# Kept orders stored in four parts, record fills and weights spread over six slots, the root's row first

## The reference

```
coeff = complex(x[...,0], x[...,1]) * sqrt_eig                  # 64 x 256 x 257
h = irfft(einsum('nlm,mlk->nkm', coeff, pct), n=512)            # 64 blocks of 256 x 512
a = layernorm(h)
key = a @ K;  logits = tanh(key @ a.T + bias) - 10000*(1-band)  # band: 12 wide
h = h + softmax(logits*temperature) @ a
f = layernorm(h)
h = h + ffn(f)      # ffn: adds one-hot results of a 7-layer net, only at rows where f[0] and f[1] are >= 0.5
```

## Time and profile before

| | us |
|---|---|
| median of three executions | 1478.48 |
| the profiled execution, its time | 1485.5 |
| its span, first to last instruction | 1483.7 |
| TensorE busy | 1341.8 (90%) |
| VectorE busy | 930.9 (63%) |
| ScalarE busy | 900.5 (61%) |
| GpSimd busy | 558.1 (38%) |
| mean granted TensorE clock | 0.962 |

### The profile page before, as it was taken

How to read it: one execution, slowest core, us unless ns; L and a number is a source line. 1 busy time by engine, 2 the same in 40 slices (tenths; PEclk the granted TensorE clock), 3 DMA queues, 4 the chain that set the end, 5 groups by cost and what they waited for, 6 DMA issues and landing times. The chain is left out here.

```text
span 1483.7 us, 30658 instructions
## 1 busy us (share of the span) xinstructions
PE 1341.8 (90%) x8813; PEld 1165.0 (79%) x8813; DVE 930.9 (63%) x2025; ACT 900.5 (61%) x1956; POOL 558.1 (38%) x1394
## 2 busy tenths in 40 slices
PE   4998877884599999999999999999999999799893
PEld 3776666674599999999999999999999988455451
DVE  1222222222488878878887887887888777566661
ACT  1222222221477777777777777777777767567661
POOL 0000000000055555555555555555555556522222
PEclk9999999997799999999999999999999999899996
DMA  9999999969423433333433333333333222100000
GB/s 353 425 422 426 424 426 425 425 266 236 92 80 98 84 82 94 94 81 84 97 82 79 96 82 81 95 86 82 89 96 79 81 55 56 35 8 8 8 3 4
DMA packets 87269, 219.64 MB, mean 148 GB/s; under 512 B 20598, under 2 KB 33538, under 8 KB 75330
## 3 DMA queue, kind: packets, MB, share of 16 engines
q1 hardware_dynamic: 77690, 190.33, 40.5%
q10 hardware_dynamic: 4160, 27.27, 4.4%
q0 software_dynamic: 5376, 1.52, 0.6%
HBM read 147.77 MB, written 72.68 MB: 149 GB/s over the span
## 5 line engine op out<-in xcount | busy, mean ns | idle before, releaser
L589 PE MATMUL ps_k<-sphi,Glo 128*128 128x256 f32 x1024 | 292.2, 285 | 0.0
L588 PE MATMUL ps_k<-splo,Ghi 128*128 128x256 f32 x1024 | 291.0, 284 | 0.0
L587 PE MATMUL ps_k<-sphi,Ghi 128*128 128x256 f32 x1024 | 288.6, 282 | 0.0
L218 PE MATMUL s1b<-pg,cg 128*128 128x256 f32 x1024 | 241.3, 395 | 47.2 <-DVE cg L190 46.1
L218 PEld LDWEIGHTS s1b<-pg,cg 128*128 128x128 f32 x1024 | 199.4, 197 | 91.6 <-issue 29.6
L190 DVE TENSOR_TENSOR cg<-xg,se 128x1024 f32<-128x1024 f32 x64 | 78.4, 1225 | 228.6 <-DMA pg<-in_pct_dram 216.5
L1196 POOL TENSOR_SCALAR ve<-var 128x2 f32<-128x2 f32 x64 | 13.9, 217 | 523.6 <-ACT squares L911 523.5
L587 PEld LDWEIGHTS ps_k<-sphi,Ghi 128*128 128x128 f32 x1024 | 194.7, 190 | 2.4
L588 PEld LDWEIGHTS ps_k<-splo,Ghi 128*128 128x128 f32 x1024 | 193.0, 189 | 2.7
L589 PEld LDWEIGHTS ps_k<-sphi,Glo 128*128 128x128 f32 x1024 | 193.8, 189 | 0.0
L273 ACT COPY stage<-s1b 128x512 f32<-128x512 f32 x104 | 60.8, 585 | 169.9 <-PE s1b L218 167.3
(11 more groups left out here) (171 smaller groups left out, 3162.1 us busy)
## 6 DMA issues: line engine op xcount, KB each, us to landing
pg<-in_pct_dram SPq DMA_DIRECT2D x64, 1024.0 KB, 26.0
xg<-in_xs_dram SPq DMA_DIRECT2D x64, 512.0 KB, 23.7
out_dram<-o SPq DMA_DIRECT2D x64, 512.0 KB
xt<-spec SPq DMA_DIRECT2D x60, 512.0 KB
spec<-stage ACTq DMA_DIRECT2D x52, 512.0 KB, 8.1
rrow<-rs SPq DMA_DIRECT2D x64, 128.0 KB
spec<-hold SPq DMA_DIRECT2D x2, 2880.0 KB, 24.9
recs<-rec SPq DMA_DIRECT2D x16, 160.0 KB, 11.6
```

Source lines behind the costliest of these rows:

```text
L218: last = nc.tensor.matmul(bank[at * PARTS + part][:, m % 2, :], cg[:, b % SETS, m * 2 + h, :], pg[:, b, m * 2 + h, :], start=(h == 0), sto ...
L587: nc.tensor.matmul(out_ap, whi, mhi, start=(j == 0), stop=False)
L588: nc.tensor.matmul(out_ap, whi, mlo, start=False, stop=False)
L589: last = nc.tensor.matmul(out_ap, wlo, mhi, start=False, stop=(j == n - 1))
```

## The change

The first load phase handles three blocks instead of four, and block 3's direct load goes behind the first `rrow` in slot 0. Blocks 4 to 7 are loaded in the direct way too (`load_direct`), in slots 0 to 3. The stores of the kept rows cover blocks 8 to 63, in four parts of 14 blocks with two DMAs each, one part in each of slots 0 to 3. The 16 fills go to slots 0, 1 and 2 (six, six, four), the seven weight loads to slots 4 and 5. The counts that are waited for on `x_loaded` and `hold_stored` follow.

```diff
+DIRECT = 8
+        def loads(n, k):
+            if isinstance(n, int) and n < DIRECT:
+                return 48 * (n // 4 + 1)
+            return n * 4 + (80 - 4 * k)
...
-            for n in range(4):
-                sp.dma_start(xt[0:FROM, n]..., spec[n]...[0:FROM]).then_inc(x_loaded[n], 16)
+            def load_direct(n, k):
+                sp.dma_start(xt[0:FROM, k]..., spec[n]...[0:FROM]).then_inc(x_loaded[k], 16)
                 for c in range(2):
-                    sp.dma_start(xt[FROM:P, n, ...], const.hold[c * NB + n:...]).then_inc(x_loaded[n], 16)
-            for c in range(2):
-                sp.dma_start(spec[4:NB, (c + 1) * NLAT - HELD * GM:(c + 1) * NLAT, :],
-                             const.hold[c * NB + 4:c * NB + NB]).then_inc(hold_stored, 16)
+                    sp.dma_start(xt[FROM:P, k, ...], const.hold[c * NB + n:...]).then_inc(x_loaded[k], 16)
+            def store_held(part):
+                each = (NB - DIRECT) // 4
+                n0 = DIRECT + part * each
+                for c in range(2):
+                    sp.dma_start(spec[n0:n0 + each, (c + 1) * NLAT - HELD * GM:(c + 1) * NLAT, :],
+                                 const.hold[c * NB + n0:c * NB + n0 + each]).then_inc(hold_stored, 16)
+            def empty_records(q0, q1):
+                empty = recs.rearrange("(p q r) w -> p q r w", p=P, r=8)
+                for q in range(q0, q1):
+                    sp.dma_start(empty[:, q], const.rec0[:, :, :]).then_inc(rec_emptied, 16)
+            for n in range(3):
+                load_direct(n, n)
             sp.wait_ge(const.rec_filled, 2)
-            empty = recs.rearrange("(p q r) w -> p q r w", p=P, r=8)
-            for q in range(NB * NLAT // (P * 8)):
-                sp.dma_start(empty[:, q], const.rec0[:, :, :]).then_inc(rec_emptied, 16)
-            for dst, src in ffn_consts:
-                sp.dma_start(dst, src).then_inc(ffn_loaded, 16)
...
                     sp.dma_start(rrow[:, k % 2], rs[i]...).then_inc(rrow_loaded[k % 2], 16)
+                if isinstance(i, int) and i == 0:
+                    load_direct(3, 3)
                 if has(i) and has(i + 4):
                     sp.wait_ge(pe_dft, i * 2 + 2)
                     sp.wait_ge(act_sphi, i + 1)
                     sp.wait_ge(dve_splo, i + 1)
-                    if isinstance(i, int) and i == 0:
-                        sp.wait_ge(hold_stored, 32)
-                    load(i + 4, k)
+                    if isinstance(i, int) and i + 4 < DIRECT:
+                        load_direct(i + 4, k)
+                    else:
+                        if isinstance(i, int) and i + 4 == DIRECT:
+                            sp.wait_ge(hold_stored, 128)
+                        load(i + 4, k)
+                if isinstance(i, int) and 0 <= i < 4:
+                    store_held(i)
+                if isinstance(i, int) and 0 <= i < 3:
+                    empty_records((0, 6, 12)[i], (6, 12, 16)[i])
+                if isinstance(i, int) and 4 <= i < 6:
+                    for dst, src in ffn_consts[(0, 4)[i - 4]:(4, 7)[i - 4]]:
+                        sp.dma_start(dst, src).then_inc(ffn_loaded, 16)
```

More of the change, by code:

```diff
@@ L519, in load @@
                              spec[n].rearrange("(h p q) w -> p h (q w)", h=2, q=2)).then_inc(x_loaded[k], 16)
-            for n in range(4):
-                sp.dma_start(xt[0:FROM, n].rearrange("p (h q) w -> p h (q w)", h=2),
-                             spec[n].rearrange("(h p q) w -> p h (q w)", h=2, q=2)[0:FROM]).then_inc(x_loaded[n], 16)
+            def load_direct(n, k):
+                sp.dma_start(xt[0:FROM, k].rearrange("p (h q) w -> p h (q w)", h=2),
+                             spec[n].rearrange("(h p q) w -> p h (q w)", h=2, q=2)[0:FROM]).then_inc(x_loaded[k], 16)
                 for c in range(2):
-                    sp.dma_start(xt[FROM:P, n, 2 * c:2 * c + 2, :].rearrange("p q w -> p (q w)"),
+                    sp.dma_start(xt[FROM:P, k, 2 * c:2 * c + 2, :].rearrange("p q w -> p (q w)"),
                                  const.hold[c * NB + n:c * NB + n + 1, :, :].rearrange("o (p q) w -> o p (q w)", q=2)
-                                 ).then_inc(x_loaded[n], 16)
-            for c in range(2):
-                sp.dma_start(spec[4:NB, (c + 1) * NLAT - HELD * GM:(c + 1) * NLAT, :],
-                             const.hold[c * NB + 4:c * NB + NB]).then_inc(hold_stored, 16)
-            sp.wait_ge(const.rec_filled, 2)
-            empty = recs.rearrange("(p q r) w -> p q r w", p=P, r=8)
-            for q in range(NB * NLAT // (P * 8)):
-                sp.dma_start(empty[:, q], const.rec0[:, :, :]).then_inc(rec_emptied, 16)
-            for dst, src in ffn_consts:
-                sp.dma_start(dst, src).then_inc(ffn_loaded, 16)
+                                 ).then_inc(x_loaded[k], 16)
+            def store_held(part):
[10 more added lines that the diff above has]
+                load_direct(n, n)
+            sp.wait_ge(const.rec_filled, 2)
             def load_records(s, u):
@@ L615, in inverse_dft @@
             def inverse_dft(n, k):
-                pe.wait_ge(x_loaded[k], n * 4 + (48 - 4 * k))
+                pe.wait_ge(x_loaded[k], loads(n, k))
                 for t in range(TILES):
@@ L823, in slot @@
                     act.wait_ge(ffn_loaded, 16 * len(ffn_consts))
-                    act.wait_ge(hold_stored, 32)
+                    act.wait_ge(hold_stored, 128)
                     nc.scalar.copy(W1h[:, :, :], const.W1f[:, :, :]).then_inc(weight_hi, 1)
@@ L852, in slot @@
                     n, k1 = i + 1, (k + 1) % 4
-                    act.wait_ge(x_loaded[k1], n * 4 + (48 - 4 * k1))
+                    act.wait_ge(x_loaded[k1], loads(n, k1))
                     wait(act, pe_logit, n - 1)
@@ L1013, in slot @@
                 if isinstance(i, int) and i == AHEAD:
-                    dve.wait_ge(hold_stored, 32)
+                    dve.wait_ge(hold_stored, 128)
                     split_weights()
```

## The result

Six executions of each: median 1486.34 us (1484.29 to 1489.4) after, 1479.76 (1477.11 to 1483.5) before, ratio 1.0044, 95% interval 1.0024 to 1.0064. The change costs 6.6 us: small, clear of noise, and just within the 0.5% that I called no change. Forecast: 1481.5, range 1455 to 1494, no change the likeliest.

A forecast was written before the change was run, and what follows sets the result against it. TensorE and VectorE wait for block 0's rrow, issued late behind stores and fills on SyncE. The 36.5 us gained at L0 are given back in slots 0 to 3, plus a 1.0 us cold slot: +3, 1481.5 us, range 1455 to 1494.

The forecast's parts named there:

- The first row: Block 0's rs and rrow go out right after its root, rs at 338.9, making its lsc 36.5 us earlier.
- L0: Start of VectorE's lsc of block 0: 383.58 before, forecast 347.1.
- The price of a part: Slots 0 to 3: two stores of 14 adjacent partitions, 7.3 us each, 14.5 us a part.
- Rival B: A part costs its bytes, 7.4 us; fills' issue sets slots 0 and 1; steps 20.3, 17.7, 13.8; 1462; chance 0.20.
- The fills: Slots 0 to 2, six, six and four: 0.53 us each moved, 2.5 us each to issue while store packets run.
- Rival D: SyncE's issue of fills, 3.1 us each, makes rs late in slots 0 and 1: +13 us, 1491.5; chance 0.13.
- The edits at nothing: Reading blocks 4 to 7 from hold, hold_stored at 128, POOL's wait for fills, waits at slot 60: no cost.
- The steps: Times between lsc of successive blocks: L1 at 372.2, then 22.9, 23.3 and 21.2 us to L4 at 439.6.
- The cold slot: One slot at the end with TensorE cold after idling: 1.0 us, 8.2 against 7.1.
- The total: The whole change: +3 us on the median, 1481.5 us.
- L1 to L4: Starts of lsc of blocks 1 to 4, where 14.8, 7.6, 9.7 and 7.4 us are given back.
- the free case: Nothing else late after the first row: L1 at 357.4, whole gain 37.5 us.

The follow-up runs named there:

- f1: Kernel before with the big stores, all 16 fills and all weights moved behind the first rs and rrow, nothing split: 1476.51 us, ratio 0.9984.
- s1: Changed kernel with each store part taking every fourth block instead of 14 adjacent ones: 1460.29 us, ratio to before 0.9875.
- p0: Kernel before with nine extra stores out of hold, from different sets of partitions, each waited for before the next: 1542.7 us in one execution.
- g1: Changed kernel with fills at three a slot over slots 0 to 5 instead of six, six, four; stores unchanged: 1488.88 us, ratio 1.0057.
- b4: Changed kernel with seven strided parts, the first and block 3's load before rs, 13 fills in the loop, weights in slot 59: 1449.26 us, ratio 0.980.
- q1: Changed kernel with the same store parts and fills issued on GpSimd's queue instead of SyncE's: 1485.56 us, ratio 1.0048.
- b2: Changed kernel with seven parts of every seventh block, one in each of slots 0 to 6, fills three a slot: 1461.93 us, ratio 0.9879.

## Why the prediction was right

- *The first row.* L0 = 347.1 forecast, 347.07 measured; rs at 338.3, 0.6 us before its forecast, and rrow at 341.8. f1 shows that by itself the first row gives little.
- *The price of a part*, 14.5 us instead of the 7.4 of its bytes. This decided, and s1 and p0 show it apart from everything else. It rested on two packets of 1.81 us among those of 3.7. The parts took 15.1 to 15.5 us; in the first the packets of the first store were over after 8.0 us. Rival B's time, 1462, is near the 1460.3 of s1, where a part takes nearly as long as B gave it (7.7 to 8.2 us against 7.4), but its path was another one: it had lsc of block 1 at 369.5 by dearer fills, and s1 had it at 364.3.
- *The fills*, 0.53 us each beside the stores. g1 took half of them out of slots 0 and 1 and was 0.8 us ahead at block 1 (1.1 at block 0) and gained nothing at block 4, less than the 2 us that I expected: it issues three in slot 3, where the changed kernel has none. In the first two slots rrow followed the last store packet by 3.6 and 3.2 us, against 4.7 and 5.2 with six fills: 0.5 us for each fill less.
- *Rival D* was closer than its chance says. It was to decide from 2.3 us a fill, and the fills took 2.7; its sign, rs issued later than the last store packet lands, is there in slot 0 (rs at 364.99, the last packet done at 364.0) and by 0.3 us in slot 1. Only g1 shows that the two bounds lie side by side, and that rs issued earlier brings rrow no earlier.
- *The edits at nothing* held. GpSimd waited once, 9.2 us, for the fills (to 414.2), and the root that it made next, by 418.8, was still ready before SyncE came to its rs at 421.8.
- *The steps.* 25.8, 24.2, 24.1 and 22.0 us measured, 25.1, 22.9, 23.3 and 21.2 forecast: each 0.7 to 1.3 short, 3.4 in sum. From rrow's issue to the first store packet I gave 2.2 + 1 + 0.4 = 3.6 us, and it was 3.6, 3.7 and 3.5 in slots 1 to 3; in slot 0, with two loads, it was 7.1 against 5.9. From the last store packet to rrow's issue it was 4.7, 5.2, 5.2 and 2.8 against 4.7, 4.7, 5.1 and 3.0. The term that was too small is the part itself, by 0.6, 0.9, 1.0 and 0.6 us. In slot 1 its first packet starts at 372.3, most others of the first store at 373.3 to 374.5, while packets of the direct load still run. A direct load reads 48 KB out of one single partition, twice: by p0's price an estimated 1.8 us each on one way. I took it for bytes like any others. That this is what delays the part is argued, not tried.
- *The cold slot*, 1.0 us at the end, didn't come: the step from block 4 to block 5 was 13.46 us, shorter than 13.76, although TensorE's granted clock was 0.75 in it. TensorE had done the next keys (until 441.1) while lsc of block 4 waited.
- *The total.* +3 forecast, +6.6 measured; the trace gives +5.4 at block 4 and +3.4 over the span. The rest is within the executions' spread.
- *Slips in the working* that changed nothing: -4 to +9 around the sum is 1477.5 to 1490.5, not 1474.5; what is given back at L1 to L4 adds up from the 37.5 us of the free case, not from 36.5; B's third step adds up to 17.3, not 17.7.

## What to carry to other kernels

When a long transfer holds up a short one that a whole pipeline waits for, cutting it in parts removes the stall only if one part, with all that is queued beside it, fits the time that a turn has free; what sticks out is paid in every turn. Work that out in the queue's own time, not in bytes. A store of a few partitions should take them spread (here every fourth or seventh) and not side by side: the same bytes took half the time. And of the things to be spread, look first for those that aren't needed yet: with most fills and the weights moved to slots 7 to 59, b4 kept its lead of 36.2 us at block 5 to the end of the traced execution (1446.1 us of span against 1483.7).

## What the hardware showed that I had not expected

- A short DMA isn't safe in a queue of its own: rrow landed a median 16.5 us after issue with 48 KB packets from another queue on the same engines (q1); without them lsc started 5.0 us after rrow's issue.
- One doubled way sets the length of a whole part: eight rows on eight ways took 4.5 to 5.0 us, eight rows with two on one way up to 7.3 (b2 to b4).
- The issue of a fill on SyncE costs 0.4 us at the least and a median of 3.8 us in the changed kernel, 2.4 before, 1.8 in s1. That goes with how long a 48 KB packet takes beside it (on the mean 5.1, 3.4 and 2.8 us), not with how much is queued, which was most before. Why wasn't tried.

```profile
L548 SPq DMA_DIRECT2D recs<-rec x16: 433/3796/4881, 349.0 to 408.8; - x16
```

(changed kernel: ns least, median, most of one issue.)
